# GNN stack on one core: two weight tiles of the GCN sweep read during the build of the adjacency, nine parameter loads moved behind the count tiles

## What is computed

```python
edge_index = jnp.stack([src, dst])
x = _layernorm(x + _L0_gnn_ref(x, src, dst, edge_weight, W0, b0))   # GCN
x = _layernorm(x + _L1_gnn_ref(x, edge_index, ...))                 # GAT, 4 heads
...
def _L0_gnn_ref(x, edge_row, edge_col, edge_val, weight, b):
    msgs = edge_val[:, None] * (x @ weight)[edge_col]
    return jax.nn.relu(jax.ops.segment_sum(msgs, edge_row, num_segments=3125) + b)
```

## Time and profile before

| What | us |
|---|---|
| runs shown, median (lowest to highest of 3) | 2210.5 (2206.9 to 2212.16) |
| the profiled execution, its own time | 2211.6 |
| its span in the profile | 2209.8 |
| TensorE matmul busy in the span | 1856.7 (84%) |
| VectorE busy | 1736.5 (79%) |
| ScalarE busy | 1195.8 (54%) |
| GpSimd busy | 120.4 (5%) |
| mean rate of the DMAs | 155 GB/s |
| mean granted TensorE clock | 0.958 of full speed |

### The profile page before, as it was taken

The page is one execution under the profiler, slowest core; times in us unless marked ns, Lnnn a source line. Parts: engine busy times, 40 slices in busy tenths (PEclk is TensorE's granted clock), DMA queues, the critical chain, the costliest instruction groups (busy, mean ns, idle before and its releaser), DMA issues. The chain is left out here.

```text
span 2209.8 us, 45503 instructions
## 1 busy us (share of the span) xinstructions
PE 1856.7 (84%) x17150; PEld 1419.5 (64%) x17151; DVE 1736.5 (79%) x1784; ACT 1195.8 (54%) x2210; POOL 120.4 (5%) x225
## 2 busy tenths in 40 slices
PE   3677776799788888988888888995899999799997
PEld 2666665444566666766676666774688888655655
DVE  5999997000689999999999999977688888677276
ACT  1666665000476777767776677765666666500202
POOL 4000000000000000000000000000000000011010
PEclk9999999899999999999999999985999999899999
DMA  4799998999043144413443144324355555299194
GB/s 114 220 255 255 256 256 231 264 272 272 4 121 81 43 120 120 120 31 91 120 120 69 54 121 120 92 62 102 78 119 119 119 119 149 100 380 392 56 404 165
DMA packets 482577, 341.91 MB, mean 155 GB/s; under 512 B 322696, under 2 KB 474528, under 8 KB 475856
## 3 DMA queue, kind: packets, MB, share of 16 engines
q1 hardware_dynamic: 476864, 337.05, 55.0%
q10 hardware_dynamic: 4928, 2.20, 0.4%
q0 software_dynamic: 720, 1.77, 0.3%
HBM read 214.05 MB, written 126.94 MB: 154 GB/s over the span
## 5 line engine op out<-in xcount | busy, mean ns | idle before, releaser
L1087 ACT ACTIVATE exponentials<-gr_ps,att_cols 128x256 f32<-128x256 f32 (+1 forms) x1300 | 486.7, 492 | 177.5 <-PE gr_ps L942 175.6
L942 PE MATMUL gr_ps<-ident,gr_r 128*128 128x128 f32 (+1 forms) x2500 | 369.2, 286 | 42.4 <-DVE gr_r L1293 40.3
L975 PE MATMUL gr_ps<-exponentials,heads 128*33 128x128 f32 (+1 forms) x5000 | 368.9, 283 | 35.2 <-DVE exponentials L1299 35.2
L1299 DVE SCALAR_TENSOR_TENSOR exponentials<-exponentials,gr_count_t 128x3072 f32<-128x3072 f32 (+1 forms) x104 | 344.0, 3307 | 25.8 <-ACT exponentials L1087 24.7
L1261 DVE CUSTOM_DVE_ANT_0 gr_unread<-gr_src_rows,gr_closed 128x3125 bf16<-128x3125 f32 (+1 forms) x100 | 341.3, 3413 | 17.2 <-ACT gr_src_rows L1141 12.5
L942 PEld LDWEIGHTS gr_ps<-ident,gr_r 128*128 128x128 f32 (+1 forms) x2500 | 274.3, 145 | 124.2 <-issue 105.7
L975 PEld LDWEIGHTS gr_ps<-exponentials,heads 128*33 128x33 f32 x5000 | 258.8, 115 | 103.3 <-issue 50.5
L577 PE MATMUL bm_ps<-bm_hot 128*96 128x100 bf16 x4224 | 223.6, 210 | 99.0 <-DVE bm_hot L527 99.0
L577 PEld LDWEIGHTS bm_ps<-bm_hot 128*96 128x96 bf16 x4224 | 206.4, 124 | 116.5 <-DVE bm_hot L527 116.5
L611 ACT ACTIVATE bm_stage<-bm_ps 96x800 f32<-96x800 f32 x264 | 207.1, 830 | 115.9 <-PE bm_ps L577 108.7
L527 DVE TENSOR_TENSOR bm_hot<-bm_hot,near 128x2304 bf16<-128x2304 bf16 x132 | 179.2, 1358 | 18.9
(11 more groups left out here) (307 smaller groups left out, 1998.7 us busy)
## 6 DMA issues: line engine op xcount, KB each, us to landing
adjacency<-bm_stage SPq DMA_DIRECT2D x264, 300.0 KB, 3.4
count_pair<-adjacency SPq DMA_DIRECT2D x37, 1600.0 KB, 8.5
count_more<-count_by_source SPq DMA_DIRECT2D x30, 1600.0 KB, 8.5
count_by_source<-gr_count_t SPq DMA_DIRECT2D x12, 3200.0 KB, 17.3
gr_src_rows<-adjacency SPq DMA_DIRECT2D x20, 1600.0 KB, 15.0
count_pair<-count_by_source SPq DMA_DIRECT2D x20, 1600.0 KB, 8.5
count_more<-adjacency SPq DMA_DIRECT2D x13, 1600.0 KB, 8.4
gr_count_t<-adjacency SPq DMA_DIRECT2D x5, 1600.0 KB, 15.0
```

The source lines that it names most:

```text
L942: last = pe.transpose(ps[:, i % RINGS, c:c + n], r[0:n, slot(g, h) + j, s * P:(s + 1) * P], k.ident[0:n, 0:n])
L975: last = pe.matmul(ps[j * PAIR:j * PAIR + C + 1, 7, 0:rows(g)], heads[:, h, s, :], e[:, s, c:c + rows(g)], start=s == 0, stop=s == NT - 1, ...
L1087: last = act.activation(e[:, s, places(g, h)], ps[:, i % RINGS, c:c + w], ACT.Exp, bias=cols[:, h, s:s + 1])
L1299: dve.scalar_tensor_tensor(part, part, 1.0, count_t[:, first:last, places(g, 0)], ALU.min, ALU.mult).then_inc(weighed, 1)
```

## The change

**Early tiles.** `count_pair` is allocated from the start instead of behind the build, and weight tiles 0 and 1 are read into it during the build. SP's loop over the passes is split into pass 0, passes 1 to 16 and passes 17 to 32; at the end of each of the latter it issues one piece of tile 0, then of tile 1: 200 of 3200 columns, 128 x 2 runs of 400 bytes, 102.4 KB, 16 pieces a tile, each counted on `early_in[t]`. The rows of tile 0 are stored by lap 5, those of tile 1 by lap 10. If there are crowded windows, ScalarE reads both tiles anew behind them (`reload_early`).

**The sweep.** TensorE takes tiles 0 and 1 from `count_pair`, tiles 2 to 4 from ring slots loaded without a wait, and loops over the other 20. The first five `left` operands are one copy on GpSimd, ahead of the memset of `heads`. Waits on `gcn_used` are renumbered, as its start value of UN = 5 is gone.

**Nine loads.** `skip_w`, `vecs` and `wjoin` leave ScalarE's queue and stand on SP's behind the two count tiles, which now wait for `gcn_used` of 2.

```diff
+        PIECES = (LAPS // UNROLL - 1) // EARLY
+        PIECE = NP // PIECES
...
+            def reload_early():
+                for t in range(EARLY):
+                    act.wait_ge(k.early_in[t], PIECES * 16)
+                    load_rows(act, k.pair[:, t, :], k.weight_rs, t).then_inc(reloaded, 16)
+                act.wait_ge(reloaded, EARLY * 16)
+
...
-            each_crowded(act, redo)
+            each_crowded(act, redo, None, reload_early)
 
...
-            each_lap(sp, store)
+            def load_early(t, n):
+                sp.dma_start(k.pair[:, t, bass.ds(n * PIECE, PIECE)].rearrange("p (t h l) -> p t h l", t=1, l=SL),
+                             k.weight_rs[:, t:t + 1, bass.ds(n * (HI // PIECES), HI // PIECES)]).then_inc(k.early_in[t], 16)
+
+            with sp.Fori(0, 1) as some:
+                four_laps(store, some)
+            for t in range(EARLY):
+                with sp.Fori(1 + t * PIECES, 1 + (t + 1) * PIECES) as some:
+                    four_laps(store, some)
+                    load_early(t, some - (1 + t * PIECES))
...
-            with sp.Fori(0, NT // UN) as lap:
+            for u in range(EARLY, UN):
+                load_rows(sp, ring[u], k.weight_rs, u).then_inc(gcn_in[u], 16)
+            with sp.Fori(1, NT // UN) as lap:
                 for u in range(UN):
-                    sp.wait_ge(gcn_used, lap * UN + (u + 1))
+                    sp.wait_ge(gcn_used, lap * UN + (u + 1 - UN))
                     load_rows(sp, ring[u], k.weight_rs, lap * UN + u).then_inc(gcn_in[u], 16)
+            sp.wait_ge(gcn_used, EARLY)
             load(0, 0)
             load(0, 1)
+            sp.dma_start(k.skip_w[:], k.L1_gnn_skip_W).then_inc(next_in, 16)
+            for n, v in enumerate((k.L1_gnn_gat_bias, k.L1_gnn_skip_b, k.L1_gnn_ln_g, k.L1_gnn_ln_b)):
+                sp.dma_start(k.vecs[:, n], v.partition_broadcast(P)).then_inc(next_in, 16)
+            for n, v in enumerate((k.L2_gnn_Wq, k.L2_gnn_Wk, k.L2_gnn_Wv, k.L2_gnn_Wo)):
+                sp.dma_start(k.wjoin[:, n], v).then_inc(next_in, 16)
             each_super(sp, super_tile)
...
+            pool.tensor_copy(left, k.X[:, 0:UN, :]).then_inc(gcn_left, 1)
             pool.memset(heads[:], 1.0).then_inc(set_up, 1)
-            with pool.Fori(0, NT // UN) as lap:
+            with pool.Fori(1, NT // UN) as lap:
                 for u in range(UN):
                     t = lap * UN + u
-                    pool.wait_ge(gcn_used, t + 1)
+                    pool.wait_ge(gcn_used, t + (1 - UN))
                     pool.tensor_copy(left[:, u, :].unsqueeze(1), k.X[:, bass.ds(t, 1), :]).then_inc(gcn_left, 1)
 
...
+                def add_tile(u, tile):
+                    for b in range(NCW):
+                        last = pe.matmul(ps[:, b, 0:CW], left[:, u, :], tile[:, b * CW:(b + 1) * CW],
+                                         start=False, stop=True, skip_group_check=True)
+                    last.then_inc(gcn_used, 1)
+
                 open_sums(pe, k, ps)
-                pe.sem_inc(gcn_used, UN)
-                with pe.Fori(0, NT // UN) as lap:
+                pe.wait_ge(gcn_left, 1)
+                for t in range(EARLY):
+                    pe.wait_ge(k.early_in[t], (LAPS // UNROLL - 1) // EARLY * 16)
+                    add_tile(t, count[:, t, :])
+                for u in range(EARLY, UN):
+                    pe.wait_ge(gcn_in[u], 16)
+                    add_tile(u, ring[u])
+                with pe.Fori(1, NT // UN) as lap:
                     for u in range(UN):
-                        pe.wait_ge(gcn_in[u], lap * 16 + 16)
-                        pe.wait_ge(gcn_left, lap * UN + (u + 1))
-                        for b in range(NCW):
-                            last = pe.matmul(ps[:, b, 0:CW], left[:, u, :], ring[u][:, b * CW:(b + 1) * CW],
-                                             start=False, stop=True, skip_group_check=True)
-                        last.then_inc(gcn_used, 1)
+                        pe.wait_ge(gcn_in[u], lap * 16 if u < EARLY else lap * 16 + 16)
+                        pe.wait_ge(gcn_left, lap * UN + (u + 2 - UN))
+                        add_tile(u, ring[u])
 
...
-            act.dma_start(k.skip_w[:], k.L1_gnn_skip_W).then_inc(next_in, 16)
-            for n, v in enumerate((k.L1_gnn_gat_bias, k.L1_gnn_skip_b, k.L1_gnn_ln_g, k.L1_gnn_ln_b)):
-                act.dma_start(k.vecs[:, n], v.partition_broadcast(P)).then_inc(next_in, 16)
-            for n, v in enumerate((k.L2_gnn_Wq, k.L2_gnn_Wk, k.L2_gnn_Wv, k.L2_gnn_Wo)):
-                act.dma_start(k.wjoin[:, n], v).then_inc(next_in, 16)
             act.wait_ge(set_up, 3)
             act.wait_ge(watt_step, 3)
...
-            act.wait_ge(gcn_used, UN + NT)
+            act.wait_ge(gcn_used, NT)
...
-            dve.wait_ge(gcn_used, UN + NT)
+            dve.wait_ge(gcn_used, NT)
...
+        k.early_in = [ctx.enter_context(nc.semaphore(f"early_in{t}")) for t in range(EARLY)]
+        pair = k.pair = sb("count_pair", [P, 2, NP])
         with ExitStack() as edges:
...
         k.last_node = sb("last_node", [P, HEADS, C + 1])
-        pair = sb("count_pair", [P, 2, NP])
         with (nc.sbuf_tensor("heads", [P, HEADS, NT, C + 1], F32) as heads,
```

More of the change, by code:

```diff
@@ L58 @@
 UNROLL = 4
+EARLY = 2
 DST_BITS = 12
@@ L468, in build_matrices @@
         ps = ctx.enter_context(nc.psum_tensor("bm_ps", [P, 8, BANK], F32))
-        cols_step = sem("bm_cols_step")
+        cols_step, reloaded = sem("bm_cols_step"), sem("bm_reloaded")
         used, lows, made, copied, redo_step, redo_made, redo_used, redo_copied, redo_stored = map(
@@ L481, in build_matrices, with four_laps, each_crowded @@
         MOST = LAPS * LW * NCH
+        PIECES = (LAPS // UNROLL - 1) // EARLY
+        PIECE = NP // PIECES
+        def four_laps(work, some):
+            for u in range(UNROLL):
+                work(some * UNROLL + u, u % 2, some * (UNROLL // 2) + u // 2)
         def each_lap(eng, work):
             with eng.Fori(0, LAPS // UNROLL) as some:
-                for u in range(UNROLL):
-                    work(some * UNROLL + u, u % 2, some * (UNROLL // 2) + u // 2)
+                four_laps(work, some)
         def table(eng, t, w, most):
             return eng.value_load(t[0:1, bass.ds(w, 1)], min_val=0, max_val=most)
-        def each_crowded(eng, work, prepare=None):
+        def each_crowded(eng, work, prepare=None, conclude=None):
             def inside(w, sizes):
@@ L504, in inside @@
                             inside(eng.snap(i * sizes[1] + w), sizes[1:])
+                    if conclude is not None and sizes[0] == LAPS * LW:
+                        conclude()
                     table(eng, k.first, w, NCH)
```

## The result

The changed kernel took 2192.86 us (median of 4 runs, 2190.47 to 2194.18), the kernel before 2208.7 us (4 runs) beside it: ratio 0.9932, 95% interval 0.9917 to 0.9946. That is 15.8 us less; 16.2 us were forecast, 2194.3 us. The profiled execution took 2193.66 us, its span is 2191.9 us.

A forecast was written before the change was run, and what follows sets the result against it. The prediction took VectorE to bound the build and tile loads the GCN sweep; -12.0 us for two fewer loads, -4.2 us for nine moved and 0 in the build took the 2210.5 us median to 2194.3 us, range 2190.5 to 2204 us.

The forecast's parts named there:

- (a): GCN sweep: SP loads 23 tiles instead of 25, at 6.02 us each, so 12.0 us less.
- (b): Head of the sweep: nine small loads leave it, 4.2 us less, with bounds of 0 and 6.1 us.
- The share by bytes: Head of the sweep: the nine loads carry 69% of the bytes, so 69% of the 6.1 us lost is gained.
- (c): Sweep: TensorE starts tile 0 at about 386.4 us, but still waits for the last load; the head start adds nothing.
- The 8.4 us granted to tile 0: Head of the sweep: tile 0 takes TensorE 8.4 us again, with the clock granted at 0.50.
- the margin: Sweep: the loads end later than TensorE's own pace would need, by about 6 to 8 us.
- (d): Build: the 32 pieces of early tiles cost 0 us, fitting into idle time of the rings.
- The rings idle 1.1 us: Build: the DMA rings stand idle 11 to 12% of four laps' 9.6 us, 1.1 us.
- 0.38 us: Build: one piece of 102.4 KB takes the rings 0.38 us at 272 GB/s.
- R2: Rival, build: rings are nearly full, each piece costs up to 0.38 us, 6 to 12 us in all; chance 0.12.
- R3: Rival, build: a piece costs the rings much of its latency; build grows 51 us, kernel 2245 us; chance 0.06.
- the 36 us: Build: 2.2 us of ring time a piece, beyond the idle 1.1 us, would add 36 us, giving 2230 us.

The follow-up runs named there:

- e7: The changed kernel, but TensorE waits for tile 2 to land before it starts tile 0: 2191.23 us, ratio 0.9935 to the kernel before.
- e5: The changed kernel with tiles 9, 14, 19 and 24 not loaded, tile 4's data multiplied instead, so sums are wrong: 2182.16 us, ratio 0.9888 to the kernel before.
- e1: The changed kernel with the nine small loads put back on ScalarE's queue: 2192.51 us against 2205.68 us before, ratio 0.994.
- e3: The changed kernel with every piece of the build read twice, back to back, the second time into a spare buffer: 2212.47 us against 2207.27 us before.
- e2: The kernel before the change with only the nine small loads moved to SP behind the count tiles: 2204.59 us against 2205.68 us, ratio 0.9996.
- e4: The changed kernel with every piece of the build read four times, back to back, three of them into a spare buffer: 2248.92 us against 2207.27 us before.
- e6: The changed kernel with four early tiles instead of two, in 32 pieces of 204.8 KB: 2181.31 us, ratio 0.9884 to the kernel before.
- f4: The changed kernel with four early tiles as 64 pieces of 102.4 KB, one behind each second lap: 2184.06 us, ratio 0.9896 to the kernel before.
- f3: The changed kernel with every piece read twice, the second behind the second lap except in the first pass: 2199.27 us against 2207.22 us before.

## Why the prediction was right

- **The bound.** The sweep ended with its loads: e7 starts TensorE 7 us later and neither the last load nor the sweep's end moves, e5 takes loads away and the sweep shortens.
- **(a), 12.0 us:** 12.7 us in e1. What the other 0.7 us are was not traced.
- **(b), 4.2 us of 0 to 6.1:** 3.8 us alone and 3.4 us on top of (a), in the sweep; the kernel times don't show it. The share by bytes was a guess and came out a little high. That the sum met the 16.2 us of the stage to 0.1 us is luck: (a) was 0.7 us too low and (b) 0.8 us too high. That the medians met it too (15.8 us) is luck as well, since the stages behind the sweep differ by more than 4 us between traces though their code is the same.
- **(c)** Tile 0 at 386.4 us and the last landing at 526.6 us came as written. The 8.4 us granted to tile 0 were wrong. They were read as tile 0 at 0.50 of the clock, but before the change the clock had risen by 403 us, within the tile. Now, with TensorE busy since 383.8 us, it rose at about 386.5 us, and two tiles took 11.0 us. It cost nothing, as TensorE is not the bound. For the same reason the margin was 10 us (e5), not 6 to 8.
- **(d), 0 us:** the build ended 0.2 us later, so the sum held, but its working did not. "The rings idle 1.1 us" and "0.38 us" a piece left room for two pieces; e3 shows 22 us for two together. Two things were wrong. The idle time was too high: it takes 1.05 for the share of full rings, while the most that a build held over 100 to 350 us was 274 GB/s at 0.98, against 256 GB/s before: by these rates an estimated 0.6 us of four laps. And I had not costed the burst: I had compared SP's time only with the length of a lap, at 0.32 us an issue, but three issues in a row hold SP for 1.9 us, and what stands between two stores holds back the stores, and with them the ring, the slot, ScalarE and TensorE. One piece a pass stays just below that edge; nothing in the working placed it there.
- **A sign that misled:** I had named over 20 us of ScalarE's waits for stores, and a build that ends later than 378.5 us, as signs of R2 or R3. The first came (37.9 us; in e1 and e7, with the same build, it was 14.0 and 20.0 us) without the second: the build ended at 377.9 us.
- **R3 and the fixed cost:** with one piece a pass nothing of it showed: 0.2 us, against the 36 us that followed from taking the fixed cost in the Trainium skill ("DMA: Bandwidth & Descriptors", Anatomy of one DMA) as time of the rings. That section gives its fit for DMAs issued from GpSimd, and these go out on SP, which the prediction did not say. In a burst a 6.4 KB DMA costs nearly as much as a piece of 102.4 KB (0.54 us of build each, against 57.2 / 96 = 0.60 us), so an issue has a fixed price there, but by SP's queue and not by the rings.

## What to carry to other kernels

Where a stage is bound by its stream of loads, the gain of loads taken out of it is about their number times the spacing of the stream (12.7 us for two at 6.02 us), until the compute's own pace is the bound (10.1 us further here), and an earlier start of the compute counts for nothing. Small loads at the head of the stream can cost more than their bytes: 3.4 to 3.8 us for nine of 64 KB, which at 272 GB/s would be an estimated 2.2 us. Before transfers are hidden in a stage whose own stores are paced by a small ring of slots, add up what one queue issues between two of its stores: one extra issue for every eight stores was free here, two together cost 22 us, and the same two spread 4 us. Read small parts of a change from the stage and not from the kernel's time.

## What the runs showed of the hardware beside this

Two things differ between runs without an edit of their own. Behind the sweep TensorE pauses, and the clock falls to 0.50 in every run, but for different lengths. In windows of 5 us, the change, then e1:

```profile
547.50:552.50 5.00, 2.82 (x12) 2.42 (x12) 3.98 (x19) 1.06 (x1) 0.00 (x0) 0.50 0.00 0
552.50:557.50 5.00, 4.47 (x19) 4.50 (x20) 4.14 (x20) 0.58 (x2) 0.00 (x0) 0.52 0.00 0
```

```profile
550.50:555.50 5.00, 2.82 (x12) 2.42 (x12) 3.94 (x18) 1.11 (x1) 0.00 (x0) 0.55 0.00 0
555.50:560.50 5.00, 4.05 (x32) 3.85 (x32) 4.14 (x20) 1.83 (x7) 0.00 (x0) 1.00 0.00 0
```

The second window behind the pause is at 0.52 in one and 1.00 in the other, and from ScalarE's first copy to its second `gr_closed` the change took 38.4 us and e1 36.3 us. The kernel before took 38.5 us, e2 36.3 us. Over all 14 traces the distance was 36.3 to 40.9 us. It was 36.3 us in the five in which the clock was back to 0.75 or more in the stretch from 18 to 21 us behind the first copy (e1, e2, e4, e6, f4), and 37.8 us or more in the nine in which it was still 0.50. So 2 to 4 us of a span can hang on when the clock returns. The other: a piece's issue on SP lasts longer beside more traffic, a median of 0.45 us with the change and 0.76 us in f3. The rings carried 274 GB/s in f3, but the second piece of each pair in e3 took 0.70 us at 258 GB/s, so full rings alone are not shown to be the cause.
